# A transformer layer on eight cores: products of quarters from unit 3 instead of unit 4, with the weight sums moved in VectorE's order

## The reference

```python
x = x + _layernorm(attn(_layernorm(x), Wq, Wk, Wv, Wo))
y = _layernorm(x)
gate = y @ (w_gate / 127).T        # w_gate: 3072 x 1024, int32
up = y @ (w_up / 127).T            # w_up: 3072 x 1024, int32
x = x + _layernorm((silu(gate) * up) @ (w_down / 127).T)
```

## Time and profile before

| | |
|---|---|
| median of three runs | 2260.64 us (2255.87 to 2260.96) |
| profiled execution | 2264.37 us |
| its span, slowest core (core 5) | 2262.7 us |
| spans of the eight cores | 2240.3 to 2262.7 us |
| PE busy | 2182.8 us, 96% of the span |
| DVE busy | 1370.1 us, 61% |
| ACT, POOL busy | 753.5 us, 324.4 us |
| weight loads with a cast, by the program | 24 in unit 0, 16 each in units 1 to 3; 512 KB each in bf16 |

### The profile page before, as it was taken

How to read it: one execution, slowest core, us unless ns; L and a number is a source line. 1 busy time by engine, 2 the same in 40 slices (tenths; PEclk the granted TensorE clock), 3 DMA queues, 4 the chain that set the end, 5 groups by cost and what they waited for, 6 DMA issues and landing times.

```text
span 2262.7 us, 41699 instructions; the slowest of 8 cores (2240.3 to 2262.7 us)
## 1 busy us (share of the span) xinstructions
PE 2182.8 (96%) x12704; PEld 1234.4 (55%) x12704; DVE 1370.1 (61%) x2477; ACT 753.5 (33%) x1151; POOL 324.4 (14%) x782
## 2 busy tenths in 40 slices
PE   5899999999999999999999999999999999999997
PEld 2444444344456565665656656565665656556573
DVE  6544543544547667585766758567575766758452
ACT  3323223132233333324333343333423343333321
POOL 4222021021010202012020110203011020200100
PEclk9999999999999999999999999999999999999999
DMA  9998867878558475685847658477675847657470
GB/s 190 145 198 166 199 138 156 213 157 184 166 131 261 113 235 165 187 249 149 252 110 234 195 153 264 115 229 182 208 216 136 259 100 246 174 170 217 118 232 38
DMA packets 292760, 410.20 MB, mean 181 GB/s; under 512 B 137792, under 2 KB 141888, under 8 KB 292544
## 3 DMA queue, kind: packets, MB, share of 16 engines
q1 hardware_dynamic: 157568, 325.13, 46.2%
q0 software_dynamic: 16128, 52.44, 14.6%
q10 hardware_dynamic: 118848, 29.98, 7.2%
HBM read 378.09 MB, written 52.43 MB: 190 GB/s over the span
## 4 chain that ended last, share of the span: by engine, by line
PE 74%; DVE 11%; DMA 5%; issue 5%; ACT 2%; ACTq 1%; POOL 1%; DVEq 1%; SPq 0%; POOLq 0%
PE pf L802 26%; PE pf L704 12%; PE pf L715 10%; PE pa L596 7%; PE pf L688 5%; PE pf L692 5%; PE pa L704 5%; PE pa L661 2%; DVE bn L885 2%; DMA scr_s<-stage 1%; DVE bn L886 1%; DVE uw L1027 1%; DMA gu<-wgu 1%; DVE x L953 1%; PE pf L814 1%
## 5 line engine op out<-in xcount | busy, mean ns | idle before, releaser
L802 PE MATMUL pf<-wd_sb,h 128*128 128x512 bf16 x2976 | 644.9, 379 | 4.5 <-DVE h L1041 4.5
L802 PEld LDWEIGHTS pf<-wd_sb,h 128*128 128x128 bf16 x2976 | 290.2, 98 | 355.7 <-issue 7.6
L704 PE MATMUL pf<-xs,gu 128*128 128x256 bf16 x3072 | 384.3, 273 | 0.0
L715 PE MATMUL pf<-xT,gu 128*128 128x512 bf16 x1536 | 362.8, 379 | 0.2 <-DMA gu<-scr_gu 0.2
L704 PEld LDWEIGHTS pf<-xs,gu 128*128 128x128 bf16 x3072 | 298.7, 98 | 62.0 <-issue 12.6
L445 POOL TENSOR_SCALAR stats<-stats 128x1 f32<-128x1 f32 (+2 forms) x158 | 50.8, 321 | 1616.4 <-DVE stats L888 1599.2
L715 PEld LDWEIGHTS pf<-xT,gu 128*128 128x128 bf16 x1536 | 149.4, 98 | 158.8 <-issue 1.0
L1111 DVE TENSOR_TENSOR x<-y,x 128x1024 f32<-128x1024 f32 x64 | 78.4, 1225 | 220.6 <-ACT y L1392 220.6
L1352 ACT ACTIVATE silu<-uw 128x256 bf16<-128x256 f32 x192 | 80.0, 417 | 356.4 <-DVE uw L1027 232.3
L596 PE MATMUL pa<-xT,wqkv_sb 128*128 128x512 bf16 x736 | 175.9, 386 | 3.8 <-ACT xT L1277 1.5
L968 DVE TENSOR_TENSOR h<-silu,pf 128x512 bf16<-128x512 bf16 x96 | 66.0, 687 | 160.2 <-PE pf L692 118.5
(11 more groups left out here) (98 smaller groups left out, 2675.7 us busy)
## 6 DMA issues: line engine op xcount, KB each, us to landing
gu<-scr_s SPq DMA_DIRECT2D x672, 256.0 KB, 4.1
gu<-scr_gu SPq DMA_DIRECT2D x192, 256.0 KB, 3.8
x<-x SPq DMA_DIRECT2D x64, 512.0 KB, 6.0
out<-x SPq DMA_DIRECT2D x64, 512.0 KB, 5.3
gu<-wgu POOLq DMA_DIRECT2D x48, 512.0 KB, 11.5
wqkv_sb<-wqkv POOLq DMA_DIRECT2D x12, 512.0 KB, 8.5
gux<-wgu POOLq DMA_DIRECT2D x12, 512.0 KB, 9.6
wd_sb<-wd POOLq DMA_DIRECT2D x24, 256.0 KB, 29.9
```

What stands on the lines that cost most here:

```text
L704: ins = eng.matmul(bank[:, 256 * g:256 * g + 256], w[:, o:o + 128], rhs[:, c, :], start=(i < 3 and g == 0 and c == 0), stop=(c == 3), skip ...
L715: ins = eng.matmul(bank[:], w[:, 128 * kc:128 * kc + 128], half(xT3, kc), start=(kc == 0), stop=(kc == KC - 1))
L802: ins = eng.matmul(*down_step(m, kc), start=(i == 0), stop=(i == HCN - 1))
```

## The change

`ST` goes from 4 to 3, so that unit 3 is a product unit too, and units 1 and 2 are the only ones that serve pairs: four each instead of two, three and three. The loop over chunks in VectorE's program places a pair's sums one chunk later: sums 0 and 1 behind `h_mul(2m)`, 2 and 3 behind `h_mul(2m + 1)`, sum 4 behind `h_mul(2m + 2)`. (Pair 0 had this place already.) All else follows from the two tables.

```diff
-ST = 4
+ST = 3
@@
-PAIRS = {1: (2, 5), 2: (1, 4, 7), 3: (0, 3, 6)}
+PAIRS = {1: (1, 3, 5, 7), 2: (0, 2, 4, 6)}
 ORDER = [m for u in PAIRS for m in PAIRS[u]]
@@
                     for k in range(HCN):
                         h_mul(p, k)
                         for m in PAIRS.get(p, ()):
-                            late = k - max(0, 2 * m - 1)
+                            late = k - 2 * m
                             if 0 <= late < 3:
                                 for i in range(2 * late, min(5, 2 * late + 2)):
                                     quarter_sum(p, m, i)
```

## The result

The changed kernel takes 2269.51 us in the median of seven runs (2265.25 to 2272.32), the kernel before 2260.80 us in the median of four runs (2255.87 to 2263.02). The ratio is 1.0041 [1.0028, 1.0055]: **0.41% slower**. Some executions of several kernels here ran at a lower granted clock and are left out of all ratios and medians: three more of the kernel before, and among others the one that gave e4_no_hold its trace (clock 0.85 to 0.86), so that this kernel was traced once more, as e14. 2269.5 us lies above the range of 2240 to 2265 us; the rival on the slower side had 2270 us. The profiled execution takes 2267.68 us, its slowest core is core 1.

What follows compares the result with a forecast made beforehand. PE, busy 96% of the span, plus its waits was taken as the bound. -13.8 + 2.1 + 1.3 = -10.4 us from 2264.4 gave 2254.0; taking half of the runs' 3.7 us lower median, it forecast 2252 us (2247 to 2258).

Steps and rivals of the forecast that it cites:

- Unit 3 becomes a product unit: Units 3 and 4: unit 3 takes the first product unit's part, unit 4 becomes settled; 13.8 us less on core 5.
- The cast loads of unit 3 go: End of unit 2: six of 16 loads, 20 us of DMA work, go; costed at nothing by itself.
- Tight pairs: Units 1 and 2: four and a half pairs lack room for the store, five before; store waits taken as before.
- One chunk later: VectorE's sums in units 1 and 2: a landed-chunk wait goes, but slots are freed 3.45 us later.
- Unit 1 after: Unit 1's waits summed over remainder and pairs 3, 5, 7: 10.3 us against 8.2 us before.
- Unit 2 after: Unit 2's waits, pair 4 costing PE 7.8 us plus 0.8 for slower matmuls: 8.6 us against 7.3 before.
- Units 1 and 2 take the gain back: Rival: one of three extra pairs' DMA work hides, two show, 11.2 us; 2258 us, no tellable difference; chance 0.28.
- A burst behind every held slot: Rival: four held loads land late together at pairs 3, 5, 7 and 4; +9.9 us, 2270 us; chance 0.13.
- The stores are quick: Rival: stores depend on SP's own queue only, 5.5 us median, so the loop fits; -26 us, 2237 us; chance 0.13.
- The rule on queues: DMA engines alternate between queues packet by packet, so SP's stores share with POOL's casts; used for the quick-stores rival.

Runs made afterwards that it cites:

- e4_no_hold: Changed kernel with sums and quarters made from w_down's weights, so no slot is held for them (output wrong); ratio 1.0007 to the kernel before.
- e14: Second trace, one run, of the changed kernel with sums and quarters made from w_down's weights, no slot held; no ratio, units 1 and 2 took 277.1 us.
- e12: Changed kernel without the reload of the projections' weights ahead of unit 3 (output partly wrong); ratio 1.0025 to the kernel before, unit 3 137.3 us.
- e2: Kernel before with only the new order, a pair's sums one chunk later; ratio 1.0003 to the kernel before.
- e1: Changed kernel with a pair's sums back at their old place, one chunk earlier; ratio 1.0029 to the kernel before.
- e8: Changed kernel with the next unit's softmaxes ahead of the same chunk's sums in VectorE's order; ratio 1.0041 to the kernel before.
- e9: Changed kernel with no slot held (sums and quarters made from w_down's weights) and eight staging buffers; ratio 0.9969 to the kernel before.
- e5: Changed kernel with eight staging buffers for sums instead of four; ratio 1.0032 to the kernel before.

## Why the prediction was wrong

Two steps failed. Of the 20 us between the forecast change (-10.4) and the one in the mean over cores (+10.0), 13.9 us are in units 1 and 2 (+3.4 forecast, +17.3 measured) and 6.5 us in units 3 and 4 (-13.8 and -7.3).

**"Unit 3 becomes a product unit" (13.8 us): right in kind, mis-sized.** Unit 3 lost its waits and unit 4 is 134.7 us, as forecast. But the sum was made on core 5, where unit 3 took 148.2 us. The mean is 144.2, and the gain of units 3 and 4 in the mean is 7.3 us. The forecast had read 7.6 us on core 1 and stated it, and took the other core's. The slowest core of one execution is the one that had the most waits; taking its waits away makes another core the slowest. It also took the 2.8 us of a first product unit as moved with nothing new; measured, unit 3 is 138.2 us where unit 4 had been 136.0. The reload ahead of it may be a part of that (e12: 0.9 us, under what one trace can tell).

**"The cast loads of unit 3 go" (nothing by itself): not contradicted, and not tested alone.** Unit 2 still waits for its own casts, ahead of 431.49 us.

**"Tight pairs", the main step that failed.** It took the waits for stores "as before, pair by pair", and the loop with a store of at most 12.56 us from the earlier trace rows. Pair 5's store takes 17.4 us in the mean over the cores after, and took 14.2 us before, in unit 1, whose stores the forecast did not look up. In the old table pairs of one unit are six chunks apart, and now four; the casts that pair 3's slot held are let go together just as pair 5 begins to store. So what a pair costs depends on the casts beside its store, and is not a constant; without any hold a store was slow too (16.36 us in e14). The pairs that the forecast named as tight, 3, 5, 7 and 4, are the ones at whose stores DVE stands, and pair 6, which it gave nothing, stands there with 14.29 us as well.

**"One chunk later": right as a mechanism, neutral in size** (e2: 1.0003; e1 against after: unit 1 4.5 us shorter, unit 2 4.8 us longer). What it missed is that it puts pair 3's fifth sum ahead of the softmax. The order shown ahead of the prediction has it, and the sum had no term: 3.81 us and 0.9 us of a slower group (260.80, 2.77 instead of 1.89 us). In e8, with the softmax ahead, the time was lost in other waits.

**"Unit 1 after" (10.3 us): 18.4 us on the slowest core; "Unit 2 after" (8.6 us): 9.5 us.** On the mean over cores the change adds 10.1 and 7.1 us where the forecast added 2.1 and 1.3 us.

**The rivals.** "Units 1 and 2 take the gain back" had half of the mechanism: DMA work. It let one of three extra pairs hide, on a DMA share of 0.71 over all of unit 1, an average that says nothing of the stretch around pairs 3 to 7; all three in full at 5.6 us are 16.8 us, and 17.3 us were measured. That the two agree is luck: e9 takes 11.8 us away with all bytes in place. "A burst behind every held slot" gave 2270 us and a decision point of 7.0 us a pair: the bursts are there in the rows (four casts at 257.13), and units 1 and 2 gave back more than unit 3 brings. But that its +9.9 us meets the +10.0 us in the mean is luck as well: it has +23.7 us for units 1 and 2 where 17.3 were measured, and the -13.8 us that were 7.3, and the two errors cancel. Removing the bursts alone (e4) gave back 4.0 to 7.7 us. "The stores are quick" fell: e5 takes the waits for the stores away and gets 2.7 us.

**The rule on queues.** Why a small store is slow beside casts, the queues say. The stretch from 262 to 272 us on core 1 of the changed kernel, within pair 5's store (packets, MB, share):

```profile
q0 software_dynamic: 346, 1.28, 92.8%
q1 hardware_dynamic: 344, 0.34, 12.0%
```

The two queues move the same number of packets, but a packet of the cast queue takes 10 x 16 x 0.928 / 346 = 0.43 us of an engine and one of the other queue 0.06 us, so SP's stores get about a ninth of the engines' time. It is so on six of the eight cores in this stretch (on cores 2 and 5 the casts end sooner, and the other queue moves more). The Trainium skill, "DMA: Bandwidth & Descriptors", section "Queues, rings and completion order", says that an engine takes packets from its queues in turn. The trace agrees with it: 346 packets against 344. From 256 us on, two quarters, a last sum and a load of `x` of 512 KB were issued ahead of the store, 4.0 us of work at 0.8 us for 256 KB, and the four casts beside it are 4 x 3.4 = 13.6 us; with its own 0.8 us that is 18.4 us of work (an estimate), and the store took 19.00 us: it was through only when nearly all of that was. The prediction had cited the same rule and made the quick stores of it; that packets of the two queues take different times, it did not count. How much of the 23.7 us this alone makes no run shows.

## What to carry to other kernels

Before work is packed into fewer stages, add up the work of the slowest shared resource in each stage, here 16 DMA engines, and let none of it hide unless the trace shows the resource idle at that very place. Where an engine waits for a transfer, look up how long that transfer takes in the very stretch that is changed, with the traffic beside it; a median over the kernel (5.5 us here) or a row from another unit (12.56 us) says too little. Take a gain from the mean over cores, or from the second slowest, not from the core that was slowest in one execution. Where two waits release the same thing (a slot held by sums and by a store), removing one gains little (4.0 and 2.7 us of 23.7 here); test them together, and once with half the bytes, before either is called the cause.

## What was not expected of the hardware

- **A load with a cast crowds out plain transfers.** 256 KB stores landed after 12.74 to 19.00 us beside casts, and the median was 5.5 us in the earlier trace rows. Packet for packet the queues took turns (346 against 344), and by time the casts had 92.8% of the engines and the stores 12.0%.
- **ACT's queue can stand in the issue of a transpose.** What it stood for is not known. On core 1 of the changed kernel, during unit 2's down stage and the reload of the projections, one issue on ACT took 8.25 us; the others 1.2 to 1.9 us:

```profile
479.91 8.25 ACTq L1289 DMA_TRANSPOSE xT<-xh  x1
490.17 1.23 ACTq L1289 DMA_TRANSPOSE xT<-xh  x1
```

- **A wait of 6 us costs more than itself.** Behind the 6.10 us of idle time at 278 us the next two groups end 6.3 us after the first starts (284.35 to 287.71 + 2.96), and undisturbed ones 3.6 us (253.45 + 1.89 from 251.72, the two groups ahead of pair 3's wait): 2.7 us more. The granted clock in that stretch, from 280 to 290 us, was 0.66 of full speed, a mean between the two levels of 1.2 and 2.4 GHz:

```profile
280.00:290.00 10.00, 5.65 (x14) 2.08 (x15) 9.38 (x17) 0.60 (x1) 0.00 (x0) 0.66 0.68 221
```
